# One core, a gated sum and two dense layers: the last product of the output in two halves of 256 columns

## The reference

```python
def _L0_rec_ref(x, W1, b1, W2, b2):       # x: 1024 x 24 x 1024, W1: 1024 x 24, W2: 1024 x 1024
    h = jax.nn.sigmoid(jnp.einsum('bts,st->bs', x, W1) + b1)
    return h @ W2.T + b2
```

## Time and profile before

| | |
|---|---|
| Runs | 306.35 us median (306.14 to 306.36) |
| Profiled execution | 305.98 us, its span 304.2 us |
| PE busy | 256.7 us (84% of the span), 1697 matmuls |
| DVE busy | 246.7 us (81%) |
| POOL busy | 240.0 us (79%) |
| ACT busy | 57.1 us (19%) |
| DMA | 109.47 MB, mean 360 GB/s over the span |
| Mean granted clock of PE | 0.961 |

### The profile page before, as it was taken

How to read it: one execution, slowest core, us unless ns; L and a number is a source line. 1 busy time by engine, 2 the same in 40 slices (tenths; PEclk the granted TensorE clock), 3 DMA queues, 4 the chain that set the end, 5 groups by cost and what they waited for, 6 DMA issues and landing times.

```text
span 304.2 us, 4878 instructions
## 1 busy us (share of the span) xinstructions
PE 256.7 (84%) x1697; PEld 217.3 (71%) x1697; DVE 246.7 (81%) x464; ACT 57.1 (19%) x99; POOL 240.0 (79%) x109
## 2 busy tenths in 40 slices
PE   0809687898198999999789779998999989899995
PEld 0709577787094878888678658886888868788684
DVE  0306979899588968878999969999998989899953
ACT  4103213422016100010060000040151010500130
POOL 2599999305799999999993999999993997989500
PEclk9978979999789999999799979999999999999999
DMA  7999999999999999999999999999999999999103
GB/s 229 392 387 386 386 387 386 386 387 387 387 387 386 385 387 385 387 386 386 386 386 386 387 396 387 397 381 388 387 386 403 388 387 386 386 387 363 63 34 138
DMA packets 56411, 109.47 MB, mean 360 GB/s; under 512 B 3642, under 2 KB 3650, under 8 KB 56388
## 3 DMA queue, kind: packets, MB, share of 16 engines
q1 hardware_dynamic: 55792, 107.06, 95.8%
q10 hardware_dynamic: 596, 2.11, 1.7%
HBM read 104.97 MB, written 4.19 MB: 359 GB/s over the span
## 4 chain that ended last, share of the span: by engine, by line
PE 39%; POOL 23%; DMA 19%; issue 11%; DVE 3%; ACT 2%; SPq 1%; POOLq 1%; DVEq 0%; ACTq 0%
PE xbank L368 20%; PE pbank L467 14%; POOL nat L680 12%; POOL nat L672 11%; DMA ring<-in_r_x 11%; DMA nat<-in_r_x 8%; PE pbank L420 2%; PE xbank L420 2%; DVE acc L504 2%; ACT hbank L625 1%; POOLq L167 1%; PE pbank L457 1%; DVE h_lo L519 1%; ACT h_hi L620 1%; SPq L327 1%
## 5 line engine op out<-in xcount | busy, mean ns | idle before, releaser
L504 DVE SCALAR_TENSOR_TENSOR acc<-xbank,w,acc 128x256 f32<-128x256 f32 (+1 forms) x360 | 197.3, 597 | 29.6 <-PE xbank L368 25.5
L368 PE MATMUL xbank<-ident,ring 128*128 128x128 f32 x1104 | 175.8, 282 | 32.4 <-DMA ring<-in_r_x 27.2
L368 PEld LDWEIGHTS xbank<-ident,ring 128*128 128x128 f32 x1104 | 139.7, 145 | 63.2 <-DVE acc L504 17.4
L672 POOL TENSOR_TENSOR nat<-nat,w1all 128x1024 f32<-128x1024 f32 x54 | 128.1, 2378 | 36.3 <-DMA nat<-in_r_x 32.9
L680 POOL TENSOR_TENSOR nat<-nat 128x1024 f32<-128x1024 f32 x46 | 109.4, 2378 | 3.6
L467 PE MATMUL pbank<-w_hi,h_hi 128*128 128x512 f32 x112 | 52.1, 465 | 1.1 <-DVE y L538 0.9
L467 PE MATMUL pbank<-w_lo,h_hi 128*128 128x512 f32 x112 | 50.4, 450 | 0.0
L467 PE MATMUL pbank<-w_hi,h_lo 128*128 128x512 f32 x112 | 45.9, 455 | 0.0
L620 ACT ACTIVATE h_hi<-acc,b1col 128x256 fp32r<-128x256 f32 (+1 forms) x24 | 13.7, 572 | 81.5 <-DVE acc L504 81.4
L607 ACT COPY y<-pbank 128x512 f32<-128x512 f32 x16 | 9.4, 586 | 80.4 <-PE pbank L467 80.3
L467 PEld LDWEIGHTS pbank<-w_hi,h_hi 128*128 128x128 f32 x112 | 21.5, 192 | 2.5 <-ACT h_hi L620 1.3
(11 more groups left out here) (37 smaller groups left out, 94.5 us busy)
## 6 DMA issues: line engine op xcount, KB each, us to landing
ring<-in_r_x SPq DMA_DIRECT2D x44, 1024.0 KB, 12.9
nat<-in_r_x SPq DMA_DIRECT2D x54, 512.0 KB, 11.9
ring<-in_r_x SPq DMA_DIRECT2D x50, 512.0 KB, 11.7
y<-in_L_rec_W SPq DMA_DIRECT2D x2, 2048.0 KB, 11.5
out_y<-y ACTq DMA_DIRECT2D x4, 512.0 KB, 6.3
out_y<-y SPq DMA_DIRECT2D x8, 256.0 KB, 2.1
w<-in_L_rec_W SPq DMA_DIRECT2D x1, 96.0 KB, 2.5
nat<-in_L_rec_b ACTq DMA_DIRECT2D x3, 4.0 KB
```

The lines of the kernel that those rows point to most:

```text
L368: mm = pe.transpose(xbank[xbank_of(u)][:, a * P:(a + 1) * P], tile, ident[:, :])
L504: nc.vector.scalar_tensor_tensor(out=total, in0=bank, scalar=weight, in1=total, op0=ALU.mult, op1=ALU.add).then_inc(unit_added, 1)
L672: nc.gpsimd.tensor_tensor(slot, slot, row, ALU.mult).then_inc(nat_weighed, 1)
```

## The change

The fourth out of the tail (n = 3: rows 896 to 1023 of the batch, columns 512 to 1023) is made in two halves of 256 columns. The first half's sum stays in `pbank1`, the second's is in `xbank0` (`xbank[NARROW % FREE]`, which is `xbank[0]`). For c = 0, 1, 2 each part has two matmuls of 256 columns in place of one of 512; for c = 3 the first half gets its three parts and then the second. The tail then has 60 matmuls, 24 of them of 256 columns. DVE adds each half by itself as soon as its sum is closed, and SP stores each half by itself: 128 rows by 1 KB in place of 128 rows by 2 KB.

```diff
+        def last_half(half):
+            bank = tail_bank(TAIL - 1) if half == 0 else xbank[NARROW % FREE]
+            return bank[:, :BANK // 2]
...
-            for n in range(OUTS):
+            for n in range(OUTS - 1):
                 j, cols = out_half(n)
                 sp.wait_ge(y_added, added_at[LAST] + n + 1)
                 sp.dma_start(out_v[:, JT + j, cols], y[:, j, cols]).then_inc(stored, 16)
-            sp.wait_ge(stored, 16 * OUTS)
+            j, cols = out_half(OUTS - 1)
+            for half in range(2):
+                part = slice(cols.start + half * BANK // 2, cols.start + (half + 1) * BANK // 2)
+                sp.wait_ge(y_added, added_at[LAST] + OUTS + half)
+                sp.dma_start(out_v[:, JT + j, part], y[:, j, part]).then_inc(stored, 16)
+            sp.wait_ge(stored, 16 * (OUTS + 1))
...
+                if n == TAIL - 1:
+                    order = [(h, q) for h in range(2) for q in range(3)][2 * k:2 * k + 2] if last else [(0, k), (1, k)]
+                    for half, kk in order:
+                        part = slice(half * BANK // 2, (half + 1) * BANK // 2)
+                        a, w = ((h_hi, w_hi), (h_hi, w_lo), (h_lo, w_hi))[kk]
+                        if kk == 2:
+                            pe.wait_ge(h_lo_ready, first_sum[LAST] + TAIL + c + 1)
+                        if c == 0 and kk == 0 and half == 1:
+                            pe.wait_ge(unit_added, last_in_bank(NARROW % FREE, UNITS))
+                        mm = pe.matmul(last_half(half), a[:, c, j * P:(j + 1) * P],
+                                       w[:, STAGES[LAST][1] + c, cols.start + part.start:cols.start + part.stop],
+                                       start=c == 0 and kk == 0, stop=last and kk == 2)
+                        if last and kk == 2:
+                            mm.then_inc(out_summed, 1)
+                    return
...
-            for n in range(OH * CUT, OUTS):
+            for n in range(OH * CUT, OUTS - 1):
                 add_out(LAST, n, tail_bank(n - OH * CUT))
+            j, cols = out_half(OUTS - 1)
+            dve.wait_ge(part_kept, kept_at[LAST - 1] + OUTS)
+            for half in range(2):
+                part = slice(half * BANK // 2, (half + 1) * BANK // 2)
+                total = y[:, j, cols.start + part.start:cols.start + part.stop]
+                dve.wait_ge(out_summed, OUTS * LAST + OUTS + half)
+                nc.vector.tensor_tensor(total, last_half(half), total, ALU.add).then_inc(y_added, 1)
```

## The result

The changed kernel took 306.83 us (median of 18 runs, 306.54 to 307.19), the kernel before 306.37 us beside it (18 runs, 306.14 to 306.73). The ratio is 1.0014, 95% interval 1.0007 to 1.0020: slower by 0.46 us, clear of noise and within the 0.2% that the prediction called the same. The forecast was +0.17 us, 306.5.

The account below looks back on a forecast made before the run. x reads bound until about 281 us, then TensorE's tail and queued stores. Tail +0.12, wait 0, adds 0, store +0.05 sum to +0.17 us: 306.35 to 306.5, likeliest 306.3 to 306.8, whole range 306.0 to 307.1.

Parts of the forecast that it names:

- the likeliest case: The forecast of 306.5 us for the whole kernel, own range 306.3 to 306.8, chance 0.67.
- What bounds the kernel: Reading x bounds up to about 281 us; then TensorE paces the tail, and four tail stores queue on busy engines.
- Tail, +0.12: TensorE, c = 0 to 2: nine matmuls become eighteen short ones, adding 0.12 us before the first tail sum closes.
- p: Distance of two short matmuls on TensorE in the tail, taken as 0.12 us; a pair's extra price is 2p - 0.227.
- The rival by the weight loads: TensorE tail: weight loads keep short matmuls from standing at 0.12 us; 307.2 to 308.4 us, chance 0.11.
- The new wait, 0: Second half's first matmul waits for the last unit in `xbank0`; up to +0.02 us, taken as 0.
- Adds: VectorE's last two adds: halves start at 301.03 and 301.38, end at 301.80 us; covered by the engines, counted 0.
- Stores, +0.05: Last store in two halves: later issue hidden by the queue, engine time 0.74 us against 0.70, rounded to +0.05.
- the high end of +0.70: Upper bound of the store term: each 1 KB packet of the last stores as dear as one of 2 KB.
- The rival of dear packets: Last stores: engines charge a 1 KB packet like one of 2 KB, +0.70 + 0.12, 307.2 us; chance 0.04.
- The rival by latency: Last store pays by latency, not by the queue; the end comes some 0.1 us earlier, 306.25 us; chance 0.15.
- The third sign: The prediction is wrong if anything before 289 us moves by more than 0.3 us.

Follow-up runs that it names:

- the first trace: The profiled execution of the changed kernel, compared with the profile of the kernel before; it took 306.94 us.
- the second trace: Trace of the changed kernel run again with no edit, beside the kernel before: 306.51 us against 306.18, ratio 1.0012.
- the new order: Changed kernel, tail reordered: c = 2 and 3 out by out for the first three outs, whole fourth out last; 305.99 us against 306.30 for the kernel before.

## Why the prediction was right, and where its sum was not

The direction was right, and so was the verdict: a little slower, within 0.2%, inside the whole range (306.0 to 307.1). But 306.83 us lies just above 306.8, the top of the likeliest case's own range. The sum, +0.17, was too small: the traces show +0.48 and +0.40, and the medians +0.46 and +0.33. Of these more than half comes from two things that the sum had at nothing. That they still fit under 0.2% is owed to their size, not to the reasoning. Step by step:

*What bounds the kernel.* Right that the loads end the part ahead and that only the tail counts. Right that in the changed kernel the last store stands behind full engines: issued 0.22 us earlier it ended no earlier. Overstated for the kernel before: there the queue held the last store back by 0.04 us, and latency and bytes tie. "The last store does not wait for its own latency alone" is true only by that little.

*Tail, +0.12.* Measured +0.22 and +0.16. The load was priced right: apart from the first pair p is 0.112 to 0.121 us, never 0.19, and a pair of halves costs 0.002 to 0.008 us more than a whole, less than my 0.013. The Trainium skill (page "TensorE: Matmul & The Clock Gate", section "LDWEIGHTS (loading the stationary operand)") gives a load of 128 columns 107 ns. The traces don't speak against it, since short ones in a row stand at 0.120 us, but no run here tells whether the load or the columns set that. The step that failed is the silent one: that the whole matmuls between the pairs keep 0.227. They lost 0.20 us in the first trace and 0.10 in the second, 0.04 of which the kernel before loses at its start as well. The rival by the weight loads needed p of 0.145 or more and fell.

*The new wait, 0.* Right in mechanism, and the wait is there to be seen. In the trace of the changed kernel VectorE's add on `xbank0`, and the load behind it:

```profile
290.45 0.47 DVE L531 SCALAR_TENSOR_TENSOR acc<-xbank,w,acc 128x256 f32<-128x256 f32 x1
290.98 0.19 PEld L441 LDWEIGHTS xbank<-w_hi,h_hi 128*128 128x128 f32 x1
```

The load starts 0.05 us behind the end of the add and 0.02 us behind the matmul before it (290.96), with which the other loads start together. With that the first pair takes 0.241 us, 0.01 more than the others (0.249 in the second trace).

*Adds.* Right in kind and nearly in size: VectorE is the bound of the last two, they start 0.61 and 0.33 us behind one another (0.60 and 0.35 said), and the last ends at +0.23 and +0.15 us, against +0.12; the excess is the tail's. One sum in it is wrong: the last half product does not enter at 300.73. Five steps of 0.12 behind the fourth out's first matmul, which stood at 300.11 and is shifted by 0.12, make 300.83. The bound of 301.16 for the add holds all the same, by luck: from the last product's entry to the add it is 0.32 us for a half (measured in the new order) and not 0.43. The time given for the 60 matmuls is short by the same 0.1 us.

*Stores, +0.05.* The mis-sized term. From the first store's issue to the last packet it is 0.11 and 0.09 us longer; and another +0.15 us lie behind the last packet, which no row of before could show and for which I had no bound on this place, though the high end of +0.70 covered it. Together 0.26 and 0.24. The rival of dear packets fell: packets of 1 KB took 47 to 49 ns against 86 for 2 KB, near my 45. The issues were 0.51 us apart instead of 0.41, at no cost behind the queue.

*The rival by latency* has a true core: where the engines are idle, a half store pays. But it pays 0.14 us, not 0.35. The form of it by the Trainium skill (page "DMA: Bandwidth & Descriptors", section "Anatomy of one DMA — SWDGE (gpsimd) path"), 2.0 us and the bytes over 436 GB/s, would give 0.30; the page states it for transfers issued by GpSimd, and these are issued by SyncE. Measured are 2.06 us for 256 KB and 1.91 for 128 KB on idle engines.

So the expected gain (0.27 us of add, 0.35 of transfer) went this way: the add's share was lost to VectorE being still at the third out, since the sums close 0.68 us apart and a whole add keeps it for 0.60. The transfer's share was lost to the full engines, where the bytes of both halves still lie ahead of the end. On top came 0.24 to 0.26 us for splitting the store, and 0.16 to 0.22 us on TensorE. With the sums spread out in time, and all short matmuls in one block, the same halves gain 0.24 us over the same order without them.

*The signs.* Short matmuls at 0.145 or more did not come, nor idle engines between the last stores. The third sign did: in the first trace VectorE's instructions stand 0.34 to 0.56 us later from 112 us on, while x is still being read, where 0.3 was allowed. In the second trace it is 0.13 us at the tail. As said above, the tail's start moves by as much and more between executions that are the same up to there, so the sign was set too tight and tells nothing about the change.

What stays open: what resets the matmul's spacing, and why the slow stretch is anything from 1 to 9 long; and why the release of a half store comes 0.15 us later.

## What to carry to other kernels

Cutting the last piece shortens the end only if the stages behind it are idle when it comes: look at the distance at which the last sums close, and compare it with an add's and a store's occupancy, before halving anything. Reorder first, so that the last sums close apart, and then halve. Keep short and long matmuls in blocks of their own, and price a store's end by a store of that shape.

## What the runs showed of the hardware that I had not expected

- Whole matmuls of 512 columns run at 0.2267 us in a settled train, but at 0.224 to 0.236 behind the train's start or behind shorter ones, for one to nine matmuls (mean 0.231 over the nine at the start of the kernel before). Those of 256 columns stand at 0.112 to 0.121 us as a pair and at 0.120 in a long row (24 in the new order).
- A store with 1 KB per row is released 0.54 to 0.57 us behind its last packet, whether it is alone, one of two, or on ScalarE's queue; one with 2 KB per row 0.39 to 0.42, also when it has only 64 rows.
- The issue of a half-width store lasts 0.45 to 0.47 us instead of 0.33 when it begins 0.38 to 0.51 us behind another store's issue, and 0.55 to 0.59 for 64 rows, also 0.68 us behind another; a pair of 64-row stores costs 0.89 us at the end of the kernel.
